# Two transformer layers on one core: a step's attention scores in three stretches of matmuls, where there were four

## The reference

```python
scores = jnp.einsum('bqhd,bkhd->bhqk', q, k) * scale   # layer 1: -inf above the diagonal
attn = jax.nn.softmax(scores, axis=-1)
out = jnp.einsum('bhqk,bkhd->bqhd', attn, v)
```

## Time and profile before

| | |
|---|---|
| median of 3 runs | 332.77 us (331.02 to 333.44) |
| the profiled execution's own time | 331.46 us |
| its span, first to last instruction | 329.7 us |
| around the span | 1.8 us |
| mean granted clock of TensorE | 0.955 of full speed |
| busy in the span | PE 281.9, DVE 263.6, ACT 207.4, POOL 205.6 us |

### The profile page before, as it was taken

The page is one execution under the profiler, slowest core; times in us unless marked ns, Lnnn a source line. Parts: engine busy times, 40 slices in busy tenths (PEclk is TensorE's granted clock), DMA queues, the critical chain, the costliest instruction groups (busy, mean ns, idle before and its releaser), DMA issues.

```text
span 329.7 us, 9464 instructions
## 1 busy us (share of the span) xinstructions
PE 281.9 (85%) x3194; PEld 199.3 (60%) x3194; DVE 263.6 (80%) x1007; ACT 207.4 (63%) x428; POOL 205.6 (62%) x326
## 2 busy tenths in 40 slices
PE   7989989997989989888997887988898888898763
PEld 3667555654666446554675456766676666666553
DVE  4897887879588888899679697687899999965565
ACT  2576865776857668496986569666385757536110
POOL 0549994471348447583779785697769756457332
PEclk9999969999899999999999799997799999899978
DMA  6684250303030220404022130403114040000000
GB/s 229 251 248 158 81 195 3 129 0 129 3 112 18 61 101 18 145 8 139 18 64 99 33 130 6 136 23 99 65 27 153 1 146 4 19 2 17 18 16 32
DMA packets 20495, 25.84 MB, mean 78 GB/s; under 512 B 3744, under 2 KB 14304, under 8 KB 20320
## 3 DMA queue, kind: packets, MB, share of 16 engines
q1 hardware_dynamic: 20016, 24.72, 22.4%
q10 hardware_dynamic: 432, 0.53, 0.5%
HBM read 6.36 MB, written 1.05 MB: 22 GB/s over the span
## 4 chain that ended last, share of the span: by engine, by line
PE 42%; DVE 32%; issue 12%; ACT 7%; POOL 4%; DMA 1%; POOLq 0%; ACTq 0%; DVEq 0%
PE bank L600 13%; DVE mx L824 7%; DVE room_c L832 6%; PE bank L615 4%; PE bank L398 4%; PE bank L388 4%; ACT E L728 3%; PE bank L465 3%; DVE turned L923 2%; PE bank L482 2%; DVE room_a L893 2%; DVE room_c L858 2%; PE bank L556 2%; PE bank L567 2%; DVE mx L832 2%
## 5 line engine op out<-in xcount | busy, mean ns | idle before, releaser
L728 ACT ACTIVATE E<-bank 128x512 f32<-128x512 f32 (+1 forms) x256 | 120.3, 550 | 78.4 <-PE bank L411 41.5
L824 DVE TENSOR_REDUCE mx<-bank 128x2 f32<-128x512 f32 x128 | 78.9, 679 | 9.3 <-PE bank L388 9.2
L832 DVE CUSTOM_DVE_ANT_0 room_c<-bank,mask_sb 128x256 f32<-128x256 f32 (+1 forms) x256 | 72.7, 349 | 1.3 <-PE bank L388 1.1
L398 PE MATMUL bank<-QK 32*128 32x256 f32 x480 | 55.8, 316 | 18.5 <-DVE hid L860 6.8
L388 PE MATMUL bank<-QK 32*128 32x256 f32 x480 | 56.8, 313 | 8.1 <-DVE mx L832 2.6
L600 PE MATMUL bank<-E,V 128*32 128x256 f32 (+1 forms) x1024 | 60.7, 383 | 0.1
L398 PEld LDWEIGHTS bank<-QK 32*128 32x128 f32 x480 | 36.9, 188 | 29.3 <-issue 21.8
L388 PEld LDWEIGHTS bank<-QK 32*128 32x128 f32 x480 | 37.2, 187 | 23.3 <-issue 8.9
L1052 POOL TENSOR_SCALAR_AFFINE_SELECT E<-E 128x512 f32<-128x512 f32 x64 | 39.2, 638 | 11.4 <-ACT E L728 11.3
L600 PEld LDWEIGHTS bank<-E,V 128*32 128x32 f32 x1024 | 31.5, 117 | 23.5 <-issue 7.0
L923 DVE STREAM_TRANSPOSE turned<-bank 128x256 f32<-128x256 f32 x32 | 14.3, 446 | 21.8 <-PE bank L600 21.8
(11 more groups left out here) (127 smaller groups left out, 558.7 us busy)
## 6 DMA issues: line engine op xcount, KB each, us to landing
spread_qk<-parts SPq DMA_DIRECT2D x30, 256.0 KB, 2.5
spread_qk<-parts SPq DMA_DIRECT2D x60, 128.0 KB, 2.1
room_c<-room_c SPq DMA_DIRECT2D x64, 32.0 KB, 1.9
xb<-x_nat SPq DMA_DIRECT2D x1, 1024.0 KB, 6.9
out<-ln_g SPq DMA_DIRECT2D x7, 128.0 KB, 1.9
xt<-x_t SPq DMA_DIRECT2D x1, 768.0 KB, 6.7
wi<-wi_all SPq DMA_DIRECT2D x1, 576.0 KB, 4.4
room_c<-fac_u SPq DMA_DIRECT2D x1, 508.0 KB, 6.5
```

What stands on the lines that cost most here:

```text
L398: nc.tensor.matmul(g_bank["exp", m][:, c * T:(c + 1) * T - q0], both[:, 1, c * P:(c + 1) * P], both[:, 0, q0:T], start=(c == 0), stop=False)
L728: act.activation(E[:, a % E_RING, j, 0:n], g_bank["exp", m][:, 0:n], ACT.Exp, scale=SCALE)\
L824: ins = nc.vector.tensor_reduce(mx[:, n % 2, :, i], bank[:, :].rearrange("p (q k) -> p q k", q=QT), AX.X, ALU.max, negate=True)
L832: ins = nc.vector.tensor_tensor_reduce(out=masked_s[:, at % 2, lo:hi], in0=bank[:, lo:hi], in1=mask_sb[:, T + lo - hi:T], scale=-1.0, scal ...
```

## The change

A step no longer calls `scores` twice. `step_scores` writes the order out:

1. banks for the maxima of g+14, g+15 and the exponentials of g, g+1 are taken, and the first stretch goes twice over four strips, as before;
2. the banks for the exponentials of g+2 and g+3 are taken, and `mt_ready` is waited for in the steps with g a multiple of 8 (before, this wait stood ahead of the first call). Then `less_maximum` of g and g+1, in strips 0 and 1, alternates with the first half of the exponentials' scores of g+2 and g+3, in strips 2 and 3; the second half of these follows;
3. the banks for the maxima of g+12 and g+13 are taken, and `less_maximum` of g+2 and g+3 alternates with the first half of the maxima's scores of g+12 and g+13; their second half follows.

The number of matmuls, their shapes, the banks and their order of readers, and everything on the other engines are the same. The maxima of the first heads and the exponentials of the last steps get functions of their own (`maxima_at_first`, `last_scores`) with the order they had.

```diff
-            def scores(maxima, exps, at):
-
-                for i, m in enumerate(maxima):
-                    take((at + i) % BANKS, ("max", m), A["max_done"], order_of(m))
-                for i, m in enumerate(exps):
-                    take((at + len(maxima) + i) % BANKS, ("exp", m), A["exp_done"], m + 1)
+            def banks_for_maxima(maxima, i):
+                for m in maxima:
+                    take(i % BANKS, ("max", m), A["max_done"], order_of(m))
+                    i += 1
...
+            def banks_for_exps(exps, i):
                 for m in exps:
-                    if m % 8 == 0:
-                        pe.wait_ge(A["mt_ready"], m // 8 + 1)
-
-                first = exps and exps[0] % QUAD == 2
+                    take(i % BANKS, ("exp", m), A["exp_done"], m + 1)
+                    i += 1
...
+            def step_scores(g, at):
+
+
+                ahead = range(g + LEAD, g + LEAD + QUAD)
+                banks_for_maxima(ahead[2:], at)
+                banks_for_exps((g, g + 1), at + 2)
                 for long in range(2):
-                    for m in exps if first else ():
+                    for m in ahead[2:]:
+                        max_scores(m, 1 - long)
+                    for m in (g, g + 1):
                         exp_scores(m, long)
-                    for m in maxima:
-                        max_scores(m, 1 - long)
-                    for m in () if first else exps:
+                banks_for_exps((g + 2, g + 3), at + QUAD + 2)
+                if g % 8 == 0:
+                    pe.wait_ge(A["mt_ready"], g // 8 + 1)
+                for i in range(2):
+                    less_maximum(g + i)
+                    exp_scores(g + 2 + i, 0)
+                for i in range(2):
+                    exp_scores(g + 2 + i, 1)
+                banks_for_maxima(ahead[:2], at + QUAD)
+                for i in range(2):
+                    less_maximum(g + 2 + i)
+                    max_scores(ahead[i], 1)
+                for i in range(2):
+                    max_scores(ahead[i], 0)
...
                 if g + LEAD < HEADS:
-                    scores((g + LEAD + 2, g + LEAD + 3), (g, g + 1), at)
-                    scores((g + LEAD, g + LEAD + 1), (g + 2, g + 3), at + QUAD)
+                    step_scores(g, at)
                 elif g < HEADS:
-                    scores((), range(g, g + QUAD), 0)
+                    last_scores(g)
```

More of the change, by code:

```diff
@@ L428, in scores, with maxima_at_first, last_scores @@
                         pe.wait_ge(A["qk_ready"], 2 * (b - 1) + m % H // 8 + 1)
+            def banks_for_exps(exps, i):
                 for m in exps:
-                    if m % 8 == 0:
-                        pe.wait_ge(A["mt_ready"], m // 8 + 1)
-                first = exps and exps[0] % QUAD == 2
+                    take(i % BANKS, ("exp", m), A["exp_done"], m + 1)
+                    i += 1
+            def maxima_at_first(maxima, at):
+                banks_for_maxima(maxima, at)
+                for c in (1, 0):
+                    for m in maxima:
+                        max_scores(m, c)
+            def step_scores(g, at):
+                ahead = range(g + LEAD, g + LEAD + QUAD)
+                banks_for_maxima(ahead[2:], at)
+                banks_for_exps((g, g + 1), at + 2)
                 for long in range(2):
-                    for m in exps if first else ():
+                    for m in ahead[2:]:
+                        max_scores(m, 1 - long)
+                    for m in (g, g + 1):
                         exp_scores(m, long)
-                    for m in maxima:
-                        max_scores(m, 1 - long)
-                    for m in () if first else exps:
+                banks_for_exps((g + 2, g + 3), at + QUAD + 2)
[12 more added lines that the diff above has]
+                    max_scores(ahead[i], 0)
+            def last_scores(g):
+                banks_for_exps(range(g, g + QUAD), 0)
+                if g % 8 == 0:
+                    pe.wait_ge(A["mt_ready"], g // 8 + 1)
+                for long in range(2):
+                    for m in range(g, g + QUAD):
                         exp_scores(m, long)
-                for m in exps:
+                for m in range(g, g + QUAD):
                     less_maximum(m)
@@ L500, in _ @@
             project(1, take(6, ("qk", 1), A["qk_out"], 2))
-            scores((2, 3), (), 0)
-            scores((0, 1), (), 2)
+            maxima_at_first((2, 3), 0)
+            maxima_at_first((0, 1), 2)
             project_group(1, 7)
             project_group(2, 0)
-            scores((6, 7), (), 4)
-            scores((4, 5), (), 6)
+            maxima_at_first((6, 7), 4)
+            maxima_at_first((4, 5), 6)
             project_group(3, 1)
             project_values(0, take(3, ("v", 0), A["v_ready"], 1))
-            scores((10, 11), (), 4)
-            scores((8, 9), (), 6)
+            maxima_at_first((10, 11), 4)
+            maxima_at_first((8, 9), 6)
             turn_maxima(0, take(2, ("mt", 0), A["mt_ready"], 1))
```

## The result

The changed kernel takes 343.55 us (median of 4 runs, 341.8 to 345.78), the kernel before 331.89 us in the same measurement (327.56 to 333.44). The medians are 11.7 us apart. The forecast was 339.0 us, +6.2 on the median shown then, with a range of 331.5 to 344. The sign and the place were right, and the size was about half of what came. The profiled execution took 345.78 us with a span of 344.0 us, 14.3 longer than before.

What follows compares the result with a forecast made beforehand. VectorE was taken to bound layer 1, VectorE and TensorE taking turns in layer 0. Terms 5.4 + 1.6 + 0.2 + 0.3 - 0.6 = 6.9 us gave 338.4 or 339.7, forecast 339.0 us; 8-in-10 range 331.5 to 344.

Steps and rivals of the forecast that it cites:

- What bounds layer 1: Layer 1: VectorE's work is the bound, 16.01 of 16.69 us a batch; TensorE counts only where VectorE waits for it.
- The fences: First claims wait for an exponential (layer 1, 0.96 us after `less_maximum`) or a maximum (layer 0); folding a stretch gains nearly nothing.
- The moved wait: Layer 1: banks of g+2, g+3 awaited before `less_maximum`; nine late steps at 0.6 us, four at 0.4, 0.2 more in step 156.
- The signs that I had named: Step 204's `less_maximum` after `hid`, L465 awaiting the exponential, VectorE idle 0.9 us before `turned`, layer 1 batch near 17.8, layer 0 unchanged.
- The step that failed: the clock: TensorE's granted clock: no term in the sum; lower clock with longer pauses appeared only in a rival, at 2 us.
- the third rival: ScalarE becomes the bound: 13 x 0.8 us plus 2 for lower clock and longer pauses, 12 us, 345; chance 0.09.
- Layer 0: Late banks delay only the second claim, 0.1 us in about seven steps, less two gains of 0.2: cost 0.3 us.
- The wait for `mt_ready`: Start of step 8: wait moves behind the first stretch, which runs in its 0.64 us of idle time; 0.6 us back.
- TensorE's time pays: Rival, both layers: a third of the folded stretch's 18 us comes through, 326.8 us; chance 0.10.
- The late exponentials are hidden: Rival, nine late steps: VectorE has other work while the PV product is late, so no change, 333.5 us; chance 0.23.
- ScalarE becomes the bound: Rival: four exponentials start only after the late banks, 0.8 us in each of thirteen steps, plus 2; 345 us; chance 0.09.
- The stretches don't overlap as written: Rival: `less_maximum` and other strips' scores don't run side by side, 4.5 us more in layer 0, 343.5 us; chance 0.05.

Runs made afterwards that it cites:

- e4: The changed kernel plus six zero-weight matmuls ahead of the wait for the banks of g+2 and g+3, in twelve late steps of layer 1: 333.67 us, ratio 1.0111.
- e10: As e5, with two zero-weight matmuls in place of six: 325.95 us, ratio 0.9808 against the kernel before.
- e1: The changed kernel with `less_maximum` of g and g+1 put ahead of the wait for the banks of g+2 and g+3: 330.97 us, ratio 0.9995.
- e3: The changed order in layer 0's steps only, the kernel before's order in layer 1: 331.16 us, ratio 1.0003.
- e6: The kernel before plus six zero-weight matmuls between the two `less_maximum` in ten late steps of layer 1: 331.49 us, ratio 0.9982.
- e11: As e6, the kernel before's four stretches, with two zero-weight matmuls in the same ten steps: 327.06 us, ratio 0.9905.
- e2: The kernel before's four stretches, with only the wait for the banks of g+2 and g+3 moved ahead of `less_maximum` of g and g+1: 345.39 us, ratio 1.0442.
- e5: e1 plus six zero-weight matmuls between the two `less_maximum` in ten late steps of layer 1: 330.78 us, ratio 0.9964.
- e12: As e4, the changed kernel, with two zero-weight matmuls ahead of the wait, in ten late steps only: 341.59 us, ratio 1.0318.

## Why the prediction was right in sign and too small

**What bounds layer 1: right.** VectorE is busy for 16.0 us of a batch in e4 and in e10 as in the earlier trace rows, and the batch's length is that and what VectorE waits for.

**The fences: right.** The stretch that was folded away gave nothing: e1 has it folded and measures 0.9995, e3 has it folded in layer 0 and measures 1.0003. The first claim waited for ScalarE's exponential of g, 0.96 us after `less_maximum` by my rule, 0.99 in the trace.

**The moved wait: right in place, a little too dear by the step.** Nine late steps at 0.6 and four at 0.4 us gave 7.0. In step 220 the claims came 0.39 and 0.49 us later than before (0.99 and 1.37 against 0.60 and 0.88), for 0.46 and 0.6 forecast: I had put a weight load in front of `less_maximum`, but its row starts 0.15 us after `hid` ends, as the old second call did. With the clock up the whole of it is 136.57 - 130.89 = 5.7 us in layer 1 (e4 against e10), where the sum had 7.2. This is rather too low: e10's clock still fell once there (183.1 to 186.5 us) and e4's not at all, and such a fall costs 1 us or a little more (below), so 5.7 to 7 us is what the runs support. The signs that I had named show the same. A batch was to take near 17.8 us, and VectorE's wait before `turned` was to grow to 0.9 us: with the clock held, in e4, they are 17.73 and 0.84, and in the changed kernel itself 20.48 and 2.12. What lies between the two pairs is the clock, and the products that hold it.

**The step that failed: the clock.** In the sum it stood at nothing, and in the third rival at 2 us, as a guess. It measured: layer 1 took 147.17 us in the changed kernel and 136.57 with the pauses filled, 10.6 us. The kernel before has such a loss as well, 135.01 against e10's 130.89, 4.1 us. The difference, 6.5 us, is what the change added; allowing for the one fall that e10 still had, it is about 5 to 6.5. (That the two parts make up the 12.2 us of layer 1 is no proof, for they are differences of the same four times.) Counting gives it a second way: ten falls cost 10.6 us, 1.06 each, and the change added six, 6.4 us. Why the clock falls at one pause and not at another stays open; that filling the pauses keeps it up is what e4 shows. I had taken the clock for a mean (0.955) and not asked when it fell. A cue stood on the page of before, whose line of the clock is below 9 in six slices of the second half, and in its step 236, where the product was slow already, at the lower level. The line, the clock by stretch and the row of the product, all of the kernel before:

```profile
PEclk9999969999899999999999799997799999899978
```

```profile
286.40:289.60 3.20, 3.20 (x36) 1.87 (x35) 1.62 (x11) 0.69 (x3) 1.23 (x2) 0.50 0.00 0
```

```profile
287.11 2.75 PE L600 MATMUL bank<-E,V 128*32 128x256 f32 x32
```

A pause that grows by the length of one delay was priced as that delay, and it should have been priced with the slow stretch behind it too: 1.28 us where the product L632 fell into it (2.79 for 1.51), 1.06 us as a mean of the ten.

**Layer 0: the forecast was -0.3 (+0.3, less the 0.6 of `mt_ready`), and most of the +1.2 us in the profile is where the clock fell.** Step 0 of the changed kernel took 1.3 us longer; part of it ran at the lower level, while the kernel before had a clock of 1.00 there (the row is the changed kernel's):

```profile
17.40:20.80 3.40, 3.40 (x36) 3.17 (x32) 2.03 (x4) 1.08 (x2) 1.03 (x2) 0.51 0.95 295
```

The order of the matmuls does not decide this: e6 has the old order in step 0 and took 5.29 us for it, with the clock down, and e3 has the changed order and took 4.20, with the clock up. Two pairs of profiles have the clock down at nearly the same three or two places of layer 0, and there the orders can be compared. From step 0 to step 128 the changed kernel took 143.85 us and e6, in the old order, 143.48; e3 took 142.65 and e11, in the old order, 142.19. So the changed order costs layer 0 some 0.4 us, where the forecast had -0.3: a small miss.

The wait for `mt_ready` ahead of step 8's first stretch was 0.64 us; in the changed kernel 0.36 us are left, ended by an exponential, so a second wait stood close behind the first and 0.28 us came back at most.

**The rivals.** *TensorE's time pays* is refuted by e1 and e3. *The late exponentials are hidden* is refuted by e4: 1.0 us a batch. *ScalarE becomes the bound* named the clock and the longer pauses, which was right, but its main term, 0.8 us of ScalarE in each of thirteen steps, came out smaller: ScalarE runs as late in e4, where 1.0 us is left of a batch with two late steps, 0.5 each. Its total of 12 us is near what came by luck, with 10.4 + 2 for some 6 to 7 and 5 to 6.5. *The stretches don't overlap as written* is refuted: the rows of step 220 have `less_maximum` at 278.22 and the next head's scores at 278.23. The Trainium skill's rule that matmuls start and end in program order ("TensorE: Matmul & The Clock Gate", Part 3) agrees with the runs: e2 issues the matmuls of the kernel before in the same order, with those of two `less_maximum` behind a wait that they don't need, and its ratio is 1.0442.

## What to carry to other kernels

A wait in an in-order queue costs what stands behind it, not what it guards; before work is interleaved, ask which wait now stands in front of the piece that others need first. Where the granted clock falls behind pauses, as here, price a longer pause with the slower work that follows it, and look in the granted clock by stretch for whether it falls already. Here two products with zeros in a pause, placed where no one waits for them, made the kernel before 1% faster (e11) and the rearranged one with its wait moved back 1.9% (e10). The rearrangement with its wait moved back was worth nothing by itself (e1, 0.9995), and so were six products (e5, 0.9964 with an interval up to 1.0001).

## What the runs showed of the hardware that I had not expected

- The granted clock fell though TensorE was busy for 4.96 of the 6.90 us before (273.40 to 280.30), with idle times of 1.32 and 0.30 us among the rest. At 0.50 of full speed the product of 32 matmuls took 2.79 us for 1.51.
- Products with zero weights hold the clock: six of them per late step, and layer 1 had 1.00 for 0.88. Two were enough in e10 (0.99) and not in e12 (0.940 over the span).
- The same kernel's times follow its clock: among the executions of the kernel before in the session of e1 to e4, the fastest took 327.42 us at a mean clock of 0.969 and the longest 336.34 us at 0.935.
- In the alternating stretch each `less_maximum` of one strip and the scores of another start within 0.01 us of each other (278.22 and 278.23), so strips do run side by side there; the time saved then ends in the next wait.
